# Issuing the quads' output stores and the zero fills from ScalarE, with a newly searched order, in a macaron layer with routed experts

## What is computed

```python
x = x + 0.5 * ffn(layernorm(x))        # A
x = x + attn(layernorm(x))
x = x + 0.5 * ffn(layernorm(x))        # B

def ffn(x):                            # x: 8192 tokens x 256
    shared = swiglu(x, ws_gate, ws_up, ws_down)           # hidden 256
    scores = sigmoid(x @ gate_weight.T)                   # 8 experts
    w, idx = top_k(scores, 2); w = 2.5 * w / w.sum(-1)
    routed = sum over the 2 chosen e of w_e * swiglu(x, w_gate[e], w_up[e], w_down[e])   # hidden 128
    return shared + routed

def attn(x):                           # per sequence; xx is x shifted by one token
    k, v, r = ((x * mix + xx * (1 - mix)) @ W.T for mix, W in k, v, r)
    state[t] = k[t] * v[t] + exp(time_decay) * state[t - 1]
    out = layernorm(r * (time_first * k * v + state)) * ln_g + ln_b
    return out @ Wo.T
```

## Time and profile before

| | |
|---|---|
| median of 3 runs | 1095.18 us (1091.2 to 1098.09) |
| the profiled execution | 1096.77 us, its span 1095.0 us |
| mean granted TensorE clock | 0.946 |
| busy: PE, DVE, ACT, POOL | 916.0, 798.9, 408.7, 700.3 us |
| DMA, share of 16 engines' span: queue of SP, queue of POOL | 50.7%, 24.4% |
| DMA queue of ACT | 864 packets, 0.12 MB |

### The profile page before, as it was taken

How to read it: one execution, slowest core, us unless ns; L and a number is a source line. 1 busy time by engine, 2 the same in 40 slices (tenths; PEclk the granted TensorE clock), 3 DMA queues, 4 the chain that set the end, 5 groups by cost and what they waited for, 6 DMA issues and landing times.

```text
span 1095.0 us, 23262 instructions
## 1 busy us (share of the span) xinstructions
PE 916.0 (84%) x7488; PEld 661.1 (60%) x7488; DVE 798.9 (73%) x2485; ACT 408.7 (37%) x737; POOL 700.3 (64%) x684
## 2 busy tenths in 40 slices
PE   1858979798889989999999989999999888969750
PEld 0526747665558567676457766567666676756640
DVE  5968655386788888899999769998987743736442
ACT  5433432344425343444443433536343323133210
POOL 2666726776787855477787668553738763665565
PEclk9979989998999999999999999999999988989885
DMA  7988979998877965466337975745335998999994
GB/s 221 273 216 187 204 179 198 204 217 201 199 191 169 209 143 144 112 159 141 102 118 163 199 189 127 160 122 121 96 94 111 243 250 219 221 226 304 196 288 134
DMA packets 337989, 198.58 MB, mean 181 GB/s; under 512 B 251728, under 2 KB 319952, under 8 KB 337872
## 3 DMA queue, kind: packets, MB, share of 16 engines
q1 hardware_dynamic: 312432, 129.84, 50.7%
q0 software_dynamic: 24576, 67.14, 24.4%
q10 hardware_dynamic: 864, 0.12, 0.1%
HBM read 47.05 MB, written 92.27 MB: 127 GB/s over the span
## 4 chain that ended last, share of the span: by engine, by line
SPq 30%; issue 16%; PE 14%; POOL 14%; DVE 13%; DMA 8%; ACT 3%; POOLq 0%; ACTq 0%; DVEq 0%
SPq L755 18%; SPq L728 7%; PE ps L1032 5%; POOL y_got L855 4%; POOL xsA L838 3%; POOL xsB L838 3%; PE ps L965 2%; SPq L763 2%; DMA y_got<-ysB,y_pos 2%; DVE acc L1257 2%; DMA xt<-rows 2%; SPq L749 2%; DVE stat L1271 2%; DMA y_got<-ysA,y_pos 2%; POOL p_exp L829 2%
## 5 line engine op out<-in xcount | busy, mean ns | idle before, releaser
L925 PE MATMUL ps<-xq,w_hi 128*128 128x128 f16 x1248 | 225.0, 225 | 37.7 <-DMA xq<-xsB 27.7
L927 PE MATMUL ps<-xq,w_hi 128*128 128x128 f16 x1248 | 225.0, 225 | 0.0
L929 PE MATMUL ps<-xq,w_lo 128*128 128x128 f16 x1248 | 224.9, 225 | 0.0
L1257 DVE SCALAR_TENSOR_TENSOR acc<-y_got,share,acc 128x256 f32<-128x256 f32 x256 | 129.9, 511 | 81.5 <-DMA y_got<-ysB,y_pos 58.8
L838 POOL DMA_INDIRECT xsB<-rows,pos x128 | 136.6, 1067 | 68.4 <-issue 34.2
L855 POOL DMA_INDIRECT y_got<-ysB,y_pos x128 | 126.8, 991 | 76.1 <-issue 38.2
L965 PE MATMUL ps<-wd,hid 128*128 x624 | 154.4, 390 | 13.1 <-ACT y_sb L1149 6.0
L855 POOL DMA_INDIRECT y_got<-ysA,y_pos x128 | 131.9, 1030 | 51.1 <-issue 43.4
L838 POOL DMA_INDIRECT xsA<-rows,pos x128 | 131.0, 1023 | 48.4 <-issue 35.9
L925 PEld LDWEIGHTS ps<-xq,w_hi 128*128 x1248 | 126.3, 101 | 47.5 <-DMA xq<-xsB 30.7
L1230 DVE SCALAR_TENSOR_TENSOR hid<-ps,hid 128x512 f32<-128x512 f32 (+1 forms) x144 | 96.6, 678 | 73.2 <-PE ps L929 49.7
(11 more groups left out here) (138 smaller groups left out, 1778.0 us busy)
## 6 DMA issues: line engine op xcount, KB each, us to landing
ysA<-y_sb SPq DMA_DIRECT2D x36, 512.0 KB, 3.8
ysB<-y_sb SPq DMA_DIRECT2D x36, 512.0 KB, 4.4
acc<-in_x_dram SPq DMA_DIRECT2D x16, 512.0 KB, 4.8
out_dram<-acc SPq DMA_DIRECT2D x16, 512.0 KB
xsA<-zeros SPq DMA_DIRECT2D x36, 128.0 KB
xsB<-zeros SPq DMA_DIRECT2D x36, 128.0 KB
acc<-in_w_chunks_dram SPq DMA_DIRECT2D x10, 256.0 KB, 5.1
xq<-xsA SPq DMA_TRANSPOSE x156
```

Of the source, the lines that this page charges most:

```text
L925: nc.tensor.matmul(half, w_hi[2 * k + b][:, cols], hi, start=(j == 0 and k == 0), stop=False, skip_group_check=True)
L927: nc.tensor.matmul(half, w_hi[2 * k + b][:, cols], lo, start=False, stop=False, skip_group_check=True)
L929: mm = nc.tensor.matmul(half, w_lo[2 * k + b][:, cols], hi, start=False, stop=(j == many - 1 and k == KC - 1), skip_group_check=True)
L1257: v.scalar_tensor_tensor(out=acc[:, s, h, :], in0=y_got[:, h, k, :], scalar=share[:, s, h, k:k + 1], in1=acc[:, s, h, :], op0=ALU.mult, op ...
```

## The change

Two tasks move from SP's list to ACT's: `y_store` and `tails`, with the same DMAs, waits and semaphores; ACT now loads the places of `tails` into its own registers. The planner's durations of three of SP's tasks are changed a little. The offsets are new: all the tables, 11 constants, and one more offset (`SHIFT`) for each single task. The planner's rules, the groups, the buffers and all arithmetic stay.

```diff
 def add(self, engine, name, key, us, urgency, after=(), lag=0.1, not_before=0.0):
-        self.not_before[name, key] = not_before
+        self.not_before[name, key] = round(not_before, 3)
...
-        self.urgency[name, key] = urgency
+        self.urgency[name, key] = round(urgency, 3)
...
-    T_LATER = (-152.5, 152.3, -373.5, 146.6, 226.3, -516.5, -68.4, -182.6, 613.3, 428.2, 615.5, -102.6, -82.4, 163.3, 33.6, 513.4)
+    T_LATER = (-17.8, -25.3, 22.2, -12.3, -10.9, 121.1, 7.3, 9.1, 68.6, 80.0, 80.1, -13.2, -46.9, -11.0, -7.9, 113.5)
...
+    SHIFT = {
+        "w_hi": (9, 13.32, -5.83, -3.48,),
...
+    }
+    shift = {name: iter(row) for name, row in SHIFT.items()}
...
-        plan.add(engine, name, key, us, urgency + LATER.get(kind, 0.0), *after, **more)
+        plan.add(engine, name, key, us, urgency + LATER.get(kind, 0.0) + next(shift[name]), *after, **more)
...
-        add("sp", "turn_rows", (f, s), 5.3, at + 10, [("row_lo", (f, s))], lag=1.6)
+        add("sp", "turn_rows", (f, s), 5.6, at + 10, [("row_lo", (f, s))], lag=1.6)
...
-        add("sp", "tails", (f, g), 5.2, at - 17, [("table", (f, g))], lag=2.0)
+        add("act", "tails", (f, g), 5.2, at - 17, [("table", (f, g))], lag=2.0)
...
-            add("sp", "fetch", (f, g, q), 1.42 * blocks_of(f, g, q), at - 10 + gap * q,
-                [("tails", (f, g)), ("table_out", (f, g))] + scattered, lag=2.2)
+            add("sp", "fetch", (f, g, q), 1.46 * blocks_of(f, g, q), at - 10 + gap * q,
+                [("tails", (f, g)), ("table_out", (f, g))] + scattered, lag=2.8)
...
-            add("sp", "y_store", (f, g, q), 0.6, at + gap * q + 9, [("evac", key)], lag=3.6)
+            add("act", "y_store", (f, g, q), 0.65, at + gap * q + 9, [("evac", key)], lag=3.6)
...
+            def y_store(f, g, q):
+                n = quad_no[f, g, q]
+                act.wait_ge(evac_done, val("evac", "E", f, g, q, per=2))
+                many = blocks_of(f, g, q)
+                act.dma_start(ys[f, g][4 * q * P:(4 * q + many) * P, :].rearrange("(j p) c -> p j c", p=P),
+                             y_sb[:, n % N_Y, 0:many]).then_inc(y_stored[n % N_Y], 16)
+
+            def tails(f, g):
+                act.wait_ge(table_done, val("table", f, g))
+                to = xs[f, g]
+                at = nc.values_load_multi_w_load_instructions(
+                    tail_at[0:1, :], engines=[mybir.EngineType.Activation], min_val=0, max_val=NE * REGION - P,
...
+                for e in range(NE):
+                    act.dma_start(to[bass.ds(at[e], P), :], zeros[:]).then_inc(tails_in, 16)
+                act.dma_start(to[NE * REGION:NE * REGION + P, :], zeros[:]).then_inc(tails_in, 16)
```

More of the change, by code:

```diff
@@ L234, in schedule @@
     plan = Plan()
-    LATER = {"bias": 191.4, "bonus": -251.7, "choose": 13.2, "combine": 566.4, "downE": -502.1, "evac": 18.4, "fetchA": 433.3, "fetchB": -144.7, "gate_upE": 370.8, "gate_upS": 265.2, "gatedE": -176.4, "gatedS": -412.0, "gatherA": 334.8, "gatherB": 453.6, "hidden_hi": -521.6, "hidden_lo": -137.2, "k_copy": -980.8, "k_proj": -627.7, "kv": 621.6, "mix": -465.9, "norm1": 3.6, "norm2": 355.5, "norm3": 687.6, "out_proj": 252.3, "out_resid": 250.3, "part": -55.7, "places": -247.3, "r_proj": -242.6, "rank": -44.8, "receive": -203.9, "resid": 241.6, "route_exp": 140.0, "router": -133.6, "row_hi": 333.7, "row_lo": -669.2, "rstd": 241.4, "rstd_o": -758.3, "scan": 227.1, "scan_turn": -970.4, "scatter": -379.0, "siluE": 633.1, "siluS": 630.7, "stats1": -44.8, "stats2": -716.1, "stats3": -71.6, "stats_o": -419.4, "store": 396.0, "table": -179.4, "table_out": -140.6, "table_turn": -578.1, "tails": -73.8, "top2": -240.3, "total": -415.7, "turn2": 340.1, "turn_rows": -211.1, "v_proj": -483.8, "weights": 128.1, "y_places": 500.4, "y_store": -272.1}
@@ L237, in schedule @@
-    T_LATER = (-152.5, 152.3, -373.5, 146.6, 226.3, -516.5, -68.4, -182.6, 613.3, 428.2, 615.5, -102.6, -82.4, 163.3, 33.6, 513.4)
-    A_LATER = (-170.4, -1218.8, 433.0, -563.5, 79.3, -253.8, 80.7, 130.1, -391.2, 22.4, -604.4, -924.4, -76.7, -266.2, -155.6, -148.7)
-    B_LATER = (-69.8, -570.3, -265.1, 204.8, 382.6, -653.7, -415.6, -333.6, -552.5, -165.4, -424.3, -464.7, 435.8, -249.4, 713.2, -146.0)
-    G_LATER = (52.1, -231.4, 329.6, 603.0, 298.4, -50.4, 403.2, -54.3)
+    LATER = {"bias": -188.2, "bonus": -42.1, "choose": -142.2, "combine": 35.9, "downE": -16.7, "evac": -221.1, "fetchA": -33.8, "fetchB": -140.3, "gate_upE": 69.6, "gate_upS": 46.6, "gatedE": -40.2, "gatedS": 107.6, "gatherA": 6.2, "gatherB": 22.5, "hidden_hi": -69.7, "hidden_lo": 57.5, "k_copy": 370.1, "k_proj": -443.1, "kv": -149.9, "mix": 5.9, "norm1": 103.2, "norm2": -128.3, "norm3": 5.4, "out_proj": -33.2, "out_resid": -73.0, "part": 35.0, "places": -94.2, "r_proj": 24.5, "rank": -171.0, "receive": -240.2, "resid": -99.6, "route_exp": -2.1, "router": -109.1, "row_hi": 44.0, "row_lo": 78.9, "rstd": 14.3, "rstd_o": -462.6, "scan": -155.5, "scan_turn": -43.3, "scatter": -56.5, "siluE": 79.1, "siluS": 70.0, "stats1": -46.9, "stats2": -125.0, "stats3": 158.6, "stats_o": -169.2, "store": 105.2, "table": -140.7, "table_out": -36.1, "table_turn": -185.3, "tails": -146.7, "top2": 272.6, "total": 25.4, "turn2": -121.3, "turn_rows": -242.8, "v_proj": -75.6, "weights": 104.4, "y_places": 270.9, "y_store": -176.9}
@@ L242, in add @@
+    shift = {name: iter(row) for name, row in SHIFT.items()}
     def add(engine, name, key, us, urgency, *after, **more):
         kind = name + key[0] if name in ("gate_up", "down", "gather", "fetch", "silu", "gated", "norm", "stats") and isinstance(key[0], str) else name
-        plan.add(engine, name, key, us, urgency + LATER.get(kind, 0.0), *after, **more)
[L246 to L256, removed]
+        plan.add(engine, name, key, us, urgency + LATER.get(kind, 0.0) + next(shift[name]), *after, **more)
+    PACE = 32.2
+    FIRST_A = 74.9
+    FIRST_T = 105.6
+    A_LEAD = 264.9
+    A_GAP = 31.7
+    E_LEAD = 19.1
+    B_LAG = 76.9
+    EB_LAG = -9.6
+    E_GAP = 10.9
+    EB_GAP = 1.7
+    G_LAG = 90.1
     t_at = {s: FIRST_T + PACE * s + T_LATER[s] for s in range(NSEQ)}
@@ L729, in turn_rows @@
                                            rows[:, n % N_ROWS, j, :]).then_inc(xt_in[n % N_XT], 16)
[L731 to L739, removed]
             def fetch(f, g, q):
@@ L757, in fetch @@
                         .then_inc(xq_in[n % N_XQ], 16)
[L759 to L764, removed]
             def store(s):
@@ L779, in load_w @@
                     sp.dma_start(to, w_chunks[c][:, GU:CW].rearrange("p (h n) -> p h n", h=2)).then_inc(wd_in[i], 16)
-            do = {"load": load, "load_w": load_w, "turn_rows": turn_rows, "tails": tails, "fetch": fetch,
-                  "y_store": y_store, "store": store}
+            do = {"load": load, "load_w": load_w, "turn_rows": turn_rows, "fetch": fetch,
+                  "store": store}
             tasks = order["sp"]
@@ L1150, in evac @@
                                    ps[:, bank_of("down", key, b), 0:many * C]).then_inc(evac_done, 1)
+            def y_store(f, g, q):
[9 more added lines that the diff above has]
+                    tail_at[0:1, :], engines=[mybir.EngineType.Activation], min_val=0, max_val=NE * REGION - P,
+                    skip_runtime_bounds_check_because="counts are at most the group's tokens")[1]
+                for e in range(NE):
+                    act.dma_start(to[bass.ds(at[e], P), :], zeros[:]).then_inc(tails_in, 16)
+                act.dma_start(to[NE * REGION:NE * REGION + P, :], zeros[:]).then_inc(tails_in, 16)
             def norm(n, s):
@@ L1196, in _ @@
             act.wait_ge(chan_in, 16)
-            do = {"w_hi": split_hi, "silu": silu, "hidden_hi": hidden_hi, "evac": evac, "norm": norm,
+            do = {"w_hi": split_hi, "silu": silu, "hidden_hi": hidden_hi, "evac": evac, "tails": tails, "y_store": y_store, "norm": norm,
                   "row_hi": row_hi, "part": part, "k_copy": k_copy, "o_bias_out": o_bias_out}
```

103 lines of the change are left out of this document (added), and 111 rows, old and new, of the table SHIFT.

## The result

The changed kernel takes 1102.4 us (median of 9 runs), the kernel before 1095.2 (9 runs) beside it: ratio 1.0072, interval 1.0047 to 1.0098. So it is no faster, and by the interval some 7 us slower. I had forecast 1040, with a range of 1005 to 1083. Where were the 62 us lost? Times in what follows are medians of all runs, ratios come from the fast runs alone, so that 1097.0 us can stand beside a ratio of 0.9969.

What follows compares the result with a forecast made beforehand. SP's issue was taken as the bound early and late, PE in the middle. From 1096.8 us, less 29.5 early and 33.5 late, plus 8 for fills on ACT, came 1041.8; runs' median 1.6 lower, so 1040, range 1005 to 1083.

Steps and rivals of the forecast that it cites:

- the late gain: Late stretch, 836 to 1054: 218 us falls to 184.5, halfway between PE's 191 and 178, a gain of 33.5 us.
- the early gain: Early stretch, 56 to 310: stores and zero fills off SP give their whole 29.5 us.
- the 0 for the order in the middle: Middle, 310 to 836: PE already works at 94%, so the new order was counted as 0 there.
- Stores off SP: SP's list: 20 early stores at 0.62 us free 12.4 us, 26 late ones 16.1 us; the 34 others give nothing.
- what is late next: After SP is relieved, early and late: PE at the middle's 94% density was taken as the next bound.
- the 1.16 of 20 us: A DMA share of 1.16 reached over 20 us, cited against the late share of 1.02 being all the engines give.
- Fills: Zero fills off SP: 17.1 us freed early, 12.8 late; on ACT 8 us of cost, bounds 0 and 46.
- the low end: Middle, new order: PE as loose as 91% would cost 16 us.
- DMA engines full: Rival, chance 0.16: late share 1.02 is the DMA engines' limit, late stays 218 us, only early shrinks: 1074 us.
- Shared issue: Rival, chance 0.08: ACT's issues slow SP's transposes by their own length, SP's 58 us come back: 1093 us.
- ACT the chain: Rival, chance 0.07: ACT's added 95 us all land in the loop of PE, SiLU and DVE: 1127 us.
- All of it PE: Rival, chance 0.12: clock 0.99 everywhere, PE 94% dense, SP freed early too, no loss on ACT: 1010 us.

Runs made afterwards that it cites:

- the small DMAs: Old order with stores on ACT, plus three small DMAs on SP where each of the 80 stores had stood, against the kernel before: 1144.0 us, ratio 1.0434.

## Why the prediction was wrong

Three terms of the sum failed: the late gain, the early gain, and the 0 for the order in the middle. By PE's busy time the changed kernel does 6.7 us more late, 10.7 more early and 15.0 less in the middle.

*Stores off SP, and what is late next.* "Each us taken from its list moves the end of the stretch, until the next bound comes" holds in the main for us added (some 50 of 75). For us taken off, the next bound was not PE at 94%, as the step "what is late next" had it, but the DMA engines, which were late already: in the old order the whole 16.1 us late came back as 20 us of slower transposes. Once the bytes of B were halved, the same move gave 16.6 us, with PE at 213.2 us early whoever stores: the late term had the right size for a stretch with room, and the early one gave nothing. The row stood in the earlier trace rows, a share of 1.02 in the late stretch. I set the 1.16 of 20 us against it as proof of room; a peak of 20 us told nothing of what 218 us give while the transposes are kept short. The rule of the Trainium skill that I weighed (DMA: Bandwidth & Descriptors, Rules for kernel authors) has two halves, and I gave the second too small a chance: issue time was a bound, as the trace agreed, and the shared engines behind it were another at the same place.

In the changed kernel itself the late stretch is lost in another way. Its 79 late transposes have a mean of 1.39 us, near the 1.35 of before, at a share of 0.77; SP waits 68.5 us there for rows that DVE hasn't made yet. So "SP is no bound in the late stretch" came true up to 934 us, yet PE doesn't decide there: the new order has the rows late. From 950 to 1054 the DMA share is 1.09, above the 1.06 of before, and 21.7 of PE's 22.5 us of late waits for `xq` lie there.

*Early,* 29.5 us for stores and fills. PE did 10.7 us more by 310 in the changed kernel, 3.7 more with the stores alone in the old order. Slower transposes don't explain that: their mean is 1.35 us in both kernels of the old order and 1.38 in the changed one. SP waits 40.3 us for DVE's rows there in the changed kernel, 0.5 before, so the freed issue stood idle; no experiment took this stretch by itself. Of the 30 us that the small DMAs add to SP early, PE loses 12 by 310 (202.7 us of PE, without them 214.7).

*Fills.* The sum had 29.9 us of gain for the fills off SP and a cost of 8 on ACT, of bounds 0 to 46. In the old order moving them alone costs 11 us net; how that divides between a gain that didn't come and a higher cost on ACT no run shows. In the new order nothing of it can be told. A SiLU queued behind nine DMAs, the named mechanism, is seen.

*The order,* taken as 0 in the middle and a help late. With all on SP it costs 22 us. It moved transposes into the middle, as the third place of the order shows, and it was the low end that I had priced: 478.05 of 526 is 91%, 16 us. I had called SP's 214 us of waits there slack and didn't ask what the moved transposes would do to the DMA share, which went from 0.59 to 0.72. That the transposes' bytes in the middle are what slows PE there fits the two pieces of 100 us above, and PE's longer waits for rows may as well come from when the new order makes the rows; no run changed either alone, so what the order loses stays open beyond these rows.

*The rivals.* "DMA engines full" named the cause that holds late in the old order, and at 1074 it was 28 us too fast, since it kept the early gain and the middle whole. "Shared issue" came nearest in time, 1093, by luck, with the wrong mechanism: the median of the transposes didn't rise, and with halved bytes, as many stores on ACT as before, the store's time on SP comes off the end. "ACT the chain" is half seen in the old order's fills. "All of it PE" isn't seen.

*The signs named ahead.* PE's late waits were to fall under 10 us: 22.5. PE was to reach 90% early and late: 87 and 86%. PE's waits for ACT were to stay under 15 us: 13.6, as forecast. The sign of an order that sets the time, a middle under 90%, was not reached (90.9%), though the order costs 22 us with all on SP. The DMA rival's sign, transposes of 2 us and more in number and a share above 1 with PE still waiting, was seen in the old order with the stores moved: 15 late transposes of 2 us and more, before 9, and 31.2 us of PE's waits for `xq`.

## What to carry to other kernels

Where a queue's sequencer and the DMA engines are both full in a stretch, moving issue time to another engine can give nothing. Here the move gave nothing, halving the bytes of B's outputs gave 13 and 16 us, and both together 29 and 32. Before issue time is moved, read the DMA share of that very stretch, and where it is near or above 1, take bytes away first. A stretch with slack on the issuing engine isn't free room for its transfers: ask what DMA share the moved transfers leave there.

## What the runs showed that I had not expected

- The same store holds ACT 0.37 us and SP 0.58 (medians of 80 each).
- At a DMA share of 0.83 to 0.86 late, no transpose on SP takes over 2.9 us; at 1.04 the longest take 6.6 and 8.1, while the median is still 1.20 in the first of these two kernels: with full DMA engines the issuing instruction itself lasts longer, so that waiting for bytes looks like issue time on SP's line. I read the earlier trace rows as issue for that reason. The Trainium skill (DMA: Bandwidth & Descriptors, Queues, rings and completion order) says that a DMA engine takes turns between the queues that have work for it; a second queue's stores slowing the first's transposes agrees in sign, 52.8 us for the 31 with the stores on ACT's queue against 42.1 with them on SP's own, but no run shows the turns.
